# Moving the first token tile's turn, one weight cut and the padding writes in a gated attention and expert kernel

## The reference, cut to what matters

```python
def reference(x, ctx, mask, g_xattn, g_ffn, ...):      # x: (4, 1024, 256) f32
    # cross attention: keys and values from ctx (64 rows, masked) and from the
    # normalised x itself (1024 rows); queries from x; 4 heads of 64
    x = x + tanh(g_xattn) * xattn(ctx, layernorm(x), mask, ...)
    t = layernorm(x)                                   # 4096 tokens
    probs = softmax(t @ w_router)                      # 8 experts
    w, idx = top_k(probs, 2)
    h = gelu(t @ w1[e] + b1[e])                        # 256 -> 1024
    y = h @ w2[e] + b2[e]                              # 1024 -> 256
    return x + tanh(g_ffn) * sum over the 2 chosen e of w[e] * y[e]
```

## Time and profile before

| | |
|---|---|
| median of 3 runs | 930.25 us (925.05 to 931.06) |
| the profiled execution | 930.25 us |
| its span, first to last instruction | 928.2 us |
| PE busy | 861.1 us, 93% of the span |
| DVE busy | 644.7 us, 69% |
| ACT busy | 513.6 us, 55% |
| POOL busy | 330.7 us, 36% |
| mean granted TensorE clock | 0.982 of full speed |
| the 16 DMA engines | 70.31 MB, mean 76 GB/s |

### The profile page before, as it was taken

How to read it: one execution, slowest core, us unless ns; L and a number is a source line. 1 busy time by engine, 2 the same in 40 slices (tenths; PEclk the granted TensorE clock), 3 DMA queues, 4 the chain that set the end, 5 groups by cost and what they waited for, 6 DMA issues and landing times.

```text
span 928.2 us, 19447 instructions
## 1 busy us (share of the span) xinstructions
PE 861.1 (93%) x5968; PEld 660.0 (71%) x5968; DVE 644.7 (69%) x1500; ACT 513.6 (55%) x1371; POOL 330.7 (36%) x241
## 2 busy tenths in 40 slices
PE   3898899999999999998989999899999999999995
PEld 3654455545455444554449999899999999999995
DVE  6757767677766767667795778675765766575695
ACT  2668676687766877558742645243433443343462
POOL 2333223332376323662144227532232223232233
PEclk8899999999999999999999999899999999999998
DMA  4801000120012201120043449352353526252272
GB/s 125 241 1 49 1 1 1 46 94 1 1 58 80 92 1 46 58 90 2 1 139 85 109 110 264 81 141 45 58 124 46 136 37 150 45 137 43 41 223 27
DMA packets 71899, 70.31 MB, mean 76 GB/s; under 512 B 18593, under 2 KB 66977, under 8 KB 71841
## 3 DMA queue, kind: packets, MB, share of 16 engines
q1 hardware_dynamic: 57696, 52.73, 19.2%
q0 software_dynamic: 13152, 16.86, 10.5%
q10 hardware_dynamic: 992, 0.00, 0.1%
HBM read 44.04 MB, written 26.31 MB: 76 GB/s over the span
## 4 chain that ended last, share of the span: by engine, by line
PE 56%; issue 13%; DVE 12%; POOL 10%; ACT 4%; DMA 2%; SPq 1%; POOLq 0%; ACTq 0%; DVEq 0%
PE psS L1665 22%; PE psF L1861 10%; PE psO L1861 10%; POOL rr L676 6%; DVE p_sum L1134 4%; POOL routed L686 3%; PE psS L1782 3%; PE psO L1798 3%; PE psF L1665 2%; PE psF L1829 2%; ACT sq L823 1%; ACT p_ring L867 1%; PE psO L1810 1%; DMA xr<-in_x 1%; DVE qkd L1108 1%
## 5 line engine op out<-in xcount | busy, mean ns | idle before, releaser
L884 ACT ACTIVATE V<-psS,b_col 128x256 f32<-128x256 f32 x280 | 116.9, 470 | 223.2 <-PE psS L1665 212.9
L694 POOL DMA_INDIRECT out<-V,token_i x70 | 121.1, 1730 | 271.1 <-DVE V L1325 246.9
L676 POOL TENSOR_TENSOR rr<-ssm,minus_half 128x4 f32<-128x4 f32 (+1 forms) x72 | 119.9, 1665 | 255.7 <-DVE ssm L1098 255.5
L867 ACT ACTIVATE p_ring<-psS,shift 128x1024 f32<-128x1024 f32 x128 | 136.5, 1111 | 72.2 <-PE psS L1782 71.8
L1798 PE MATMUL psO<-p_ring,V 128*64 128x512 f32 x576 | 148.8, 613 | 1.5 <-ACT o_sb L855 1.5
L1134 DVE TENSOR_TENSOR p_sum<-p_sum,p_ring 128x1024 f32<-128x1024 f32 (+1 forms) x112 | 136.0, 1214 | 0.6
L1861 PE MATMUL psF<-ln_hi,K 128*128 128x256 f32 x560 | 123.3, 284 | 0.0
L1782 PE MATMUL psS<-Q,K 64*128 64x512 f32 x864 | 122.6, 416 | 0.0
L1782 PEld LDWEIGHTS psS<-Q,K 64*128 64x128 f32 x864 | 77.6, 189 | 61.1 <-issue 42.9
L1861 PE MATMUL psO<-ln_hi,K 128*128 128x256 f32 x560 | 120.6, 278 | 0.0
L1304 DVE TENSOR_TENSOR K<-V,K 128x512 fp32r<-128x512 f32 x140 | 97.1, 693 | 4.8
(11 more groups left out here) (289 smaller groups left out, 1763.6 us busy)
## 6 DMA issues: line engine op xcount, KB each, us to landing
xr<-in_L_ffn_w SPq DMA_DIRECT2D x11, 1024.0 KB, 8.2
xn<-in_L_ffn_w SPq DMA_DIRECT2D x11, 1024.0 KB, 5.0
lnf<-routed SPq DMA_DIRECT2D x35, 258.0 KB
routed<-pad_rows SPq DMA_DIRECT2D x17, 258.0 KB, 9.9
xr<-in_x SPq DMA_DIRECT2D x8, 512.0 KB, 4.5
xb<-in_x SPq DMA_DIRECT2D x4, 1024.0 KB, 6.0
out<-xb SPq DMA_DIRECT2D x4, 1024.0 KB
b_raw<-in_L_ffn_b SPq DMA_DIRECT2D x11, 128.0 KB, 3.2
```

The source lines that it names most:

```text
L676: pool.tensor_tensor(rr[0:p, c % 2, n], ssm[0:p, c % 2, n], minus_half[0:p, n], ALU.pow).then_inc(rr_ready, 1)
L694: pool.indirect_dma_start(out_rows, bass.IndirectOffsetOnAxis(ap=token_i[:, m:m + 1], axis=0), y_out[:, m, :], None, bounds_check=NTOK - 1 ...
L867: act.activation(p_ring[0:p, u % RING, :], psS[u % 2][0:p].rearrange("p a n -> p (a n)"), ACT.Exp, bias=bias).then_inc(exp_done, 1)
L884: act.activation(g32[:, q % 2, (c % 2) * TM:(c % 2 + 1) * TM], psH[q][:, (c % 2) * TM:(c % 2 + 1) * TM], ACT.Gelu_apprx_tanh, bias=b1_col[ ...
```

## The change

Three moves; no instruction is added or taken out. (1) In the last window turn_tile(0) goes from the end of group 6 to the end of group 7, and turned_hi(0), turned_lo(0) and take_meta(0) from group 7 to group 8. (2) DVE's second cut of w2 goes from between the last two additions of probabilities to the end of group 8, ahead of turned_lo(0). (3) On SP load_w1(3) comes ahead of the pads, the 8 pads are split into two fours, load_w2(3) stands between them, load_rows(7) behind load_w2(3), and load_b1(3) and the second four pads behind load_rows(7).

```diff
                         yield 7 if apart else g % 2, name
-                    if w + 1 == WINDOWS and i == 6:
+                    if w + 1 == WINDOWS and i == 7:
                         yield 0, ("rows",)
...
                 load_rows(6, kept_row(6))
+                load_w1(3)
                 sp.wait_ge(pads_known, 1)
-                for e in range(NE):
+                for e in range(NE // 2):
                     pad(e)
+                load_w2(3)
                 load_rows(7, kept_row(7))
-                load_w1(3)
-                load_w2(3)
+                load_b1(3)
+                for e in range(NE // 2, NE):
+                    pad(e)
                 load_rows(8, kept_row(8))
-                load_b1(3)
...
-                        if i == 7:
+                        if i == 8:
                             turned_hi(0)
...
-                    if w + 1 == WINDOWS and i == 5:
-                        cut(w2_parts[0:1], 0, w2_ready)
+                    if w + 1 == WINDOWS and i in (5, 8):
+                        cut(w2_parts[i // 8:i // 8 + 1], i // 8, w2_ready)
...
-                    if w + 1 == WINDOWS and i == 7:
+                    if w + 1 == WINDOWS and i == 8:
                         turned_lo(0)
                         take_meta(0)
 
-                add_probabilities(2 * NG - 2)
-                cut(w2_parts[1:2], 1, w2_ready)
-                add_probabilities(2 * NG - 1)
+                for u in (2 * NG - 2, 2 * NG - 1):
+                    add_probabilities(u)
...
-                    if w + 1 == WINDOWS and i == 6:
+                    if w + 1 == WINDOWS and i == 7:
                         wait_bank_free(pe, ("rows",))
                         turn_tile(0)
```

## The result

| | before | changed |
|---|---|---|
| median | 929.92 us (925.05 to 931.3, 6 runs) | 937.97 us (937.55 to 940.14, 6 runs) |
| profiled execution, span | 930.25 us, 928.2 us | 940.48 us, 938.5 us |
| PE busy | 861.1 us | 858.3 us |
| mean granted clock | 0.982 | 0.981 |

The ratio is 1.0101, with a 95% interval of 1.0074 to 1.0129: slower, by 8 to 9 us. The profiled execution of the changed kernel is 2.5 us above its median, and above all six runs of the table; the two spans differ by 10.3 us. PE has no more to do; it waits in other places.

A forecast was written before the change was run, and what follows sets the result against it. PE, busy 93% of the span, was taken to bound the kernel, so moves count through its few gaps. SP's queue +5.9 us and the attention's end +0.2 gave +6.1 on 930.25 us: 936 us, range 928.5 to 941.

The forecast's parts named there:

- A: Main case, as worked out: rows(7) land at 581 to 586, time 932.5 to 938.5 us; chance 0.50.
- w1 can't go out earlier, and holds what is behind it: SP's queue: load_w1(3) waits for DVE's cut, so goes out no earlier than 567.3 and holds the pads.
- rows(7) out at 573.5: SP's queue: load_rows(7), behind w1, four pads, w2 and b2, is issued at about 573.5, against 566.48.
- Landing at 584, at the latest 587.2: DMA queue: rows(7) land at 584 by summed transfer work; bounds 577.4 and 587.2.
- the account: DMA work ahead of and with rows(7): SP's transfers 11.3 us, POOL's about 4.1, plus 1.0 to first bytes.
- C: Rival: as B, and PE's clock isn't lowered at the attention's end, -1.6 us: 928.3 us; chance 0.07.
- The cost is L - 578.1: Tile 7: rows(7) landing at time L cost L - 578.1; +5.9 us at 584, -0.7 and +9.1 at the bounds.
- The wait for the plan is swallowed and first_layer(7) runs at full clock: Tile 7: the 4.11 us wait vanishes, the slow clock falls beside the plan, and first_layer(7) takes 5.75 us.
- rows(8), rows(9), the rest: Tiles 8 onward: rows(8) land near 590, wanted at 599; rows(9) have 1.8 us slack; no stall, the delay stays.
- The attention's end: Moves 1 and 2: the 1.90 us wait at `sums` moves ahead of first_layer(0) as 2.4; cost +0.2 us.
- B: Rival, not slower: queue drains near its best rate, rows(7) land near 577.5 to 578, time 930 us; chance 0.28.
- D: Rival, slower: rows(7) land at 587, PE stands again ahead of first_layer(7), rows(9)'s slack is used; 941 us; chance 0.15.

The follow-up runs named there:

- e2: Move 3 alone (SP's queue), the attention's end as in the kernel before: 936.04 us against 925.73, ratio 1.0107.
- e10: Changed kernel with load_b1(3) moved behind load_rows(8), where it was before: 937.08 us against 926.28, ratio 1.0118.
- e9: Changed kernel with all 8 pads between load_w1(3) and load_w2(3), ahead of rows(7): 943.86 us against 928.07, ratio 1.0176.
- e6: Changed kernel with load_rows(7) and load_w2(3) exchanged, so rows(7) follow the first four pads: 933.19 us against 927.28, ratio 1.0061.
- e5: Changed kernel with keep_expert() ahead of plan_tiles() at tile 6: 938.65 us against 927.28 for the kernel before, ratio 1.0109.
- e4: Kernel before with keep_expert() ahead of plan_tiles() at tile 6: 926.58 us against 925.73, ratio 1.0012.
- e1: Moves 1 and 2 alone (the attention's end), SP's queue as in the kernel before: 926.42 us against 925.73, ratio 1.0009.
- e11: Kernel before with plan_tiles cut in two, first half at tile 6, rest at tile 7: 922.58 us against 926.28, ratio 0.9956.
- e3: Changed kernel with load_rows(7) directly behind load_w1(3), ahead of pads and w2: 930.86 us against 925.73, ratio 1.0051.
- e7: Kernel before with keep_expert() ahead of plan_tiles() and POOL's last four scatters ahead of add_rows(6): 931.58 us against 928.07, ratio 1.0032.

## Why the prediction was right or wrong

- **Forecast.** 936 us, range 928.5 to 941; measured 937.97. The direction, the place and the mechanism were right, the size was 6.1 us forecast and 8.1 found between the medians (10.3 between the two profiles). That the time falls into A's 932.5 to 938.5 is in part luck: the landing missed A's 581 to 586, and with the landing found the formula gives 940.9, which is the profiled execution (940.48) and not the median. I gave 0.80 to a change within 1% and 0.17 to slower by more; the ratio of 1.0101 is just beyond that edge, and e2 and e10 with 1.0107 and 1.0118 are too, so I was too sure of the first.
- **w1 can't go out earlier, and holds what is behind it.** Right: forecast 567.3, found 567.59.
- **rows(7) out at 573.5.** Found 576.13. The first pad went out 1.9 us after w1 and not 0.4 us, and w2 and b2 took 2.6 us of issuing and not 1. By itself this counts for little: the DMA engines' share was 0.99 or more in every window from 570 to 588.
- **Landing at 584, at the latest 587.2.** This is the term that was mis-sized: found 588.5, outside my own bound. The work of the DMA queues, from w1's issue to the landing, in the changed kernel and in e9:

```profile
DMA packets 5147, 5.54 MB, mean 264 GB/s; under 512 B 1498, under 2 KB 4571, under 8 KB 5147
q1 hardware_dynamic: 4379, 4.07, 76.2%
q0 software_dynamic: 768, 1.47, 25.0%
```

```profile
q1 hardware_dynamic: 4944, 4.61, 74.6%
q0 software_dynamic: 768, 1.47, 22.2%
```

  The first is 567.5 to 588.5 us, the second 566.2 to 590.9. The bound didn't fail by its rate: I had put 251 GB/s, and the mean was 264. It failed by its bytes, 5.54 MB against 4.75: POOL moved 1.47 MB and not 1.2, and SP's queue 4.07 and not 3.55, so that about 0.5 MB of what stands behind rows(7) (two pads' worth) was moved before they had landed. In e9 nothing but b1 stands behind them, and SP's bytes are those of the account (3.55 and four pads more); there the terms themselves can be seen short. POOL's transfers took 22.2% of 24.7 us = 5.5 us for my 4.1, and SP's 74.6% = 18.4 us, where the terms with all eight pads add up to 15.7. For POOL the reason is a mean over scatters and additions, 0.46 us each. In the changed kernel the additions stand alone in the queue at 560 to 564 us:

```profile
560.00:562.00 2.00, 2.00 (x19) 2.00 (x18) 1.41 (x3) 1.08 (x3) 1.70 (x2) 1.00 0.59 66
562.00:564.00 2.00, 2.00 (x21) 2.00 (x19) 1.65 (x4) 1.72 (x4) 1.47 (x2) 1.00 0.60 66
564.00:566.00 2.00, 2.00 (x20) 2.00 (x19) 1.85 (x5) 1.60 (x3) 1.62 (x2) 1.00 0.36 122
```

  (0.59 + 0.60) x 2 us is 2.4 us of work for two additions, 1.2 each, at 66 GB/s; the scatters behind them run at 122. Two additions and seven or eight scatters are then about 5 us. For SP's queue the excess seems to lie with w2, b2 and perhaps b1 more than with the pads: w2 with b2 was put at 3.1 us, and the rows came 5.5 us later from e6 to the changed kernel and 4.6 from e6 to e10; a further pad cost 1.0 us in e9. What w2 and b2 do beyond their bytes is open.
- **Two slips on the way.** The 263 GB/s that I called the rate of loaded engines was not one: in that window of the earlier trace rows their share was 0.77, and only pads were moving. And C's sum, 930.25 - 0.7 - 1.6, is 928.0, not 928.3. Neither changes the forecast.
- **The cost is L - 578.1.** Right above the break-even: the table holds it within 0.2 us over six kernels, with a zero good to about 1 us. With the landing of 588.5 put in, it gives 10.4; the profiles show 10.3.
- **The wait for the plan is swallowed and first_layer(7) runs at full clock.** Right: 0.98 us and 5.99 us, and the low clock lies in second_layer(6), where the chain showed it. It cost less there than the 2.9 us that I allowed: turn and second_layer(6) took 8.14 us against 6.32, 1.8 more.
- **rows(8), rows(9), the rest.** Right: rows(8) out at 591.17, just behind take_meta(7), and no wait at turn_tile(8) or turn_tile(9). The slack of rows(9) was smaller than the 1.8 us that I gave it: they went out at 611.51 and were wanted at 615.4, and such a load took 3.1 us in e5 and 3.3 in e4, not 2.3, which leaves an estimated 0.5 to 0.8. In e4 and e5, where PE came earlier, it was gone.
- **The attention's end.** Not contradicted: +0.2 forecast; e1 gives +0.8 with an interval from -0.2 to +1.9 us, and the profile +0.3 at turn_tile(5). The wait ahead of first_layer(0) is 2.32 us for 2.4.
- **Rivals.** B (landing by the best rate, no change) is out, and with it the estimate by the rule of the Trainium skill (DMA: Bandwidth & Descriptors, the anatomy of one DMA), 577.4 against 588.5: a fixed part and bytes at 436 GB/s, which the page gives for one DMA issued by GpSimd, don't describe a loaded queue of SP in which scattered rows and additions share the engines. C is out: the granted clock was 0.50 at 484 to 486 us, as it was at 486 to 488 in the kernel before. D had the late landing right and its second stand wrong.

## What to carry to other kernels

A load that an engine will stand for must not be put behind an issue that itself waits, nor behind transfers that nobody needs soon; work it out as the sum of what is ahead in the queue, each kind of transfer by its own measured engine time. When a wait is taken away, list everything that is behind the instruction that caused it, on its engine and on the others: in e4 the second product of the same plan gave the gain back, while cutting the plan so that PE's own work covers nearly all of each half (e11) kept it. A wait of a few us on PE costs more than itself, since the clock has to come back: 2.9 us behind a wait of 4.1 and 1.8 behind one of 14.7 here; but if another engine sets the end at that point, that part costs nothing.

## What the runs showed of the hardware that I had not expected

- A longer wait did not make the restart slower. In the changed kernel, after 14.66 us of idle time, PE restarted at 588.54 and was at full clock from about 592.6, 4.1 us later, which cost 1.8 us. In the kernel before, after 4.11 us, it restarted at 584.48 and was at full clock from about 590.4, 6.0 us later, which cost 2.9. The ends are worked out from the windows with a mean clock between the levels, 0.85 here (changed) and 0.89 (before):

```profile
592.00:594.00 2.00, 2.00 (x17) 2.00 (x16) 1.71 (x10) 0.00 (x0) 0.00 (x0) 0.85 0.51 132
```

```profile
590.00:592.00 2.00, 2.00 (x17) 2.00 (x17) 1.12 (x2) 1.14 (x3) 1.39 (x3) 0.89 0.64 70
```

- An addition into HBM from POOL takes 1.2 us of all 16 engines for 128 KB, three times a scatter of 128 rows into `routed` (0.36 x 2 us for about two of them).
- With the engines full, the issue of one DMA on SP can take long: 6.29 us for one pad in e3, and 9.13 us for four in the changed kernel, where four took 3.98 while the queue was short. What is behind on SP is then late even if nothing in the program holds it.
- PE can slow down to one matmul in 0.71 us without a wait in the program (e7). The times of that kernel spread over 9 us, and with one profile of either kind it isn't known how often this happens.
